# Picks as plain fp32 matmuls, and twelve picked slots instead of eleven, in a graph network on one core

## The reference

```python
# layer 0: two rounds of the mean over incoming edges
h = x @ W_lin + b_lin
agg1 = mean_aggregate(h, src, dst, N_NODES)          # mean of h[src] per dst
h = jnp.tanh(agg1 @ W1_agg + h @ W1_root + b1)       # 16 features
agg2 = mean_aggregate(h, src, dst, N_NODES)
out = jnp.tanh(agg2 @ W2_agg + h @ W2_root + b2)     # 64 features
# x = layernorm(x + out); layer 1: gated messages
h = x @ Wn.T + bn
w = ssp(ssp(edge_attr @ We1.T + be1) @ We2.T + be2)  # softplus - log 2
agg = segment_sum(h[src] * w, dst)
out = ssp(agg @ Wc.T + bc) @ Wp.T + bp
# result: layernorm(x + out)
```

## Time and profile before

| | |
|---|---|
| median of 3 runs | 8767.93 us (8767.54 to 8774.95) |
| profiled execution, first to last instruction | 8760.1 us (its own time beyond this span is not shown) |
| mean granted clock of TensorE | 0.951 of 2.4 GHz |
| TensorE matmuls, busy | 7637.1 us, 87% |
| GpSimd | 6259.5 us, 71% |
| ScalarE | 5860.1 us, 67% |
| VectorE | 5505.1 us, 63% |
| DMA | 392.62 MB, 45 GB/s over the span |

### The profile page before, as it was taken

How to read it: one execution, slowest core, us unless ns; L and a number is a source line. 1 busy time by engine, 2 the same in 40 slices (tenths; PEclk the granted TensorE clock), 3 DMA queues, 4 the chain that set the end, 5 groups by cost and what they waited for, 6 DMA issues and landing times. The chain is left out here.

```text
span 8760.1 us, 165117 instructions
## 1 busy us (share of the span) xinstructions
PE 7637.1 (87%) x51516; PEld 6905.6 (79%) x51517; DVE 5505.1 (63%) x7447; ACT 5860.1 (67%) x10176; POOL 6259.5 (71%) x6471
## 2 busy tenths in 40 slices
PE   7999999999989999999999777777777777888887
PEld 6999999888889999998888666666666666776775
DVE  5655656666645555556666666666666666777777
ACT  5777777666657777776666566666666666666665
POOL 5777777766557777777664477777777777777776
PEclk9999999999989999999999798988988889999999
DMA  2111112111111111111111222222222222222222
GB/s 75 35 34 35 35 34 35 31 30 28 25 40 34 35 34 35 34 34 31 31 30 23 75 56 59 55 57 57 55 58 56 55 59 55 55 59 56 55 56 59
DMA packets 341135, 392.62 MB, mean 45 GB/s; under 512 B 165119, under 2 KB 240563, under 8 KB 340564
## 3 DMA queue, kind: packets, MB, share of 16 engines
q0 software_dynamic: 204000, 151.96, 12.1%
q1 hardware_dynamic: 136750, 239.87, 8.1%
q10 hardware_dynamic: 322, 0.03, 0.0%
HBM read 375.47 MB, written 15.92 MB: 45 GB/s over the span
## 5 line engine op out<-in xcount | busy, mean ns | idle before, releaser
L699 PE MATMUL banks<-split_sb,e_low_hot 128*128 128x400 f32 x22000 | 4092.6, 346 | 45.6 <-DVE split_sb L752 45.6
L699 PEld LDWEIGHTS banks<-split_sb,e_low_hot 128*128 128x128 f32 x22000 | 4015.6, 189 | 74.1 <-DVE split_sb L752 46.1
L922 POOL DMA_INDIRECT big<-hn_table,src_i x2875 | 2857.0, 994 | 883.7 <-issue 870.7
L645 POOL DMA_INDIRECT big<-p_table,src_i x1750 | 1655.8, 946 | 695.2 <-issue 528.7
L758 DVE TENSOR_REDUCE picked<-banks 128x48 f32<-128x1200 f32 x1000 | 1300.1, 1300 | 1352.1 <-PE banks L699 1351.1
L670 ACT ACTIVATE e_low_hot<-e_key_off 128x1536 fp32r<-128x1536 f16 x1000 | 1381.1, 1381 | 1130.6 <-PE banks L699 1112.7
L645 POOL DMA_INDIRECT big<-h_table,src_i x1750 | 1674.9, 957 | 612.5 <-issue 529.6
L666 ACT ACTIVATE e_key_off<-e_key_in,node_off 128x384 f16<-128x384 f16 (+1 forms) x4000 | 2028.4, 577 | 125.5 <-DMA e_key_in<-sel_dram 41.4
L957 PE MATMUL banks<-hn_split,e_low_hot 128*128 128x448 f32 x7000 | 1500.1, 370 | 75.5 <-issue 70.1
L957 PEld LDWEIGHTS banks<-hn_split,e_low_hot 128*128 128x128 f32 x7000 | 1298.0, 188 | 217.1 <-issue 96.6
L781 DVE TENSOR_TENSOR hot<-e_dst_pair,banks 128x1536 bf16<-128x1536 bf16 (+1 forms) x934 | 931.1, 997 | 69.9 <-issue 0.6
(11 more groups left out here) (216 smaller groups left out, 4491.7 us busy)
## 6 DMA issues: line engine op xcount, KB each, us to landing
e_wide<-in_edge_t SPq DMA_DIRECT2D x125, 832.0 KB
e_key_in<-sel_dram SPq DMA_DIRECT2D x250, 343.8 KB
big<-hn_table,src_i POOLq DMA_INDIRECT x2875
big<-p_table,src_i POOLq DMA_INDIRECT x1750
big<-h_table,src_i POOLq DMA_INDIRECT x1750
e_key_in<-gate_dram SPq DMA_DIRECT2D x125, 64.0 KB
src_i<-in_src SPq DMA_DIRECT2D x375, 12.5 KB, 1.7
e_key_in<-sel_dram SPq DMA_DIRECT2D x250, 8.2 KB
```

What stands on the lines that cost most here:

```text
L645: pool.indirect_dma_start(buf[u][:, j, 0:ROW0], None, table, bass.IndirectOffsetOnAxis(ap=src_i[u][:, j:j + 1], axis=0),).then_inc(gathere ...
L699: last = pe.matmul(o, low_hot[gr][:, h, e], split_sb[:, part, h * HI1:(h + 1) * HI1, :], start=(h == 0 and part == 0), stop=(h == HI2 - 1 ...
L922: pool.indirect_dma_start(buf[u][:, j, 0:F], None, table, bass.IndirectOffsetOnAxis(ap=src_i[u][:, j:j + 1], axis=0),).then_inc(gathered[u ...
```

## The change

A pick becomes one matmul in plain fp32 where it was two in float32r. The tables are no longer split: split_sb becomes table_sb, hn_split becomes hn_all, and both are fp32. At the start of e1 and e2 the table is copied by place_table. In the normalising stage the bias addition writes into hn_all directly, the and and the subtraction on VectorE and the copy on ScalarE go, and the store to memory reads from hn_all. In e1 and e2 there are 12 picked slots, in four groups of three, and 13 gathered ones.

```diff
-SIZE = (3, 3, 3, 2)
+SIZE = (3, 3, 3, 3)
...
-        split_sb = mid.enter_context(nc.sbuf_tensor("split_sb", [P, 2, HI1 * HI2, H], F32R))
+        table_sb = mid.enter_context(nc.sbuf_tensor("table_sb", [P, HI1 * HI2, H], F32))
...
-                for part in range(2):
-                    dve.tensor_scalar(split_sb[:, part].rearrange("p (h a) f -> p h a f", h=HI2),
-                                      away[:, :, 0:HI1].unsqueeze(3).to_broadcast([P, HI2, HI1, H]),
-                                      1.0 - part, None, ALU.mult)
+                dve.tensor_copy(table_sb[:, :, :].rearrange("p (h a) f -> p h a f", h=HI2),
+                                away[:, :, 0:HI1].unsqueeze(3).to_broadcast([P, HI2, HI1, H]))
...
-            low_hot = [tiles.enter_context(nc.sbuf_tensor(f"{tag}_low_hot{gr}", [P, HI2, SIZE[gr] * P], F32R))
+            low_hot = [tiles.enter_context(nc.sbuf_tensor(f"{tag}_low_hot{gr}", [P, HI2, SIZE[gr] * P], F32))
...
-                                for part in range(2):
-                                    last = pe.matmul(o, low_hot[gr][:, h, e],
-                                                     split_sb[:, part, h * HI1:(h + 1) * HI1, :],
-                                                     start=(h == 0 and part == 0), stop=(h == HI2 - 1 and part == 1))
+                                last = pe.matmul(o, low_hot[gr][:, h, e], table_sb[:, h * HI1:(h + 1) * HI1, :],
+                                                 start=(h == 0), stop=(h == HI2 - 1))
...
-                    def split_table():
-                        tops, rests = [split_sb[0:PR, part].rearrange("p (h a) f -> p a h f", h=HI2) for part in range(2)]
-                        dve.wait_ge(split_in, 32)
-                        scratch = h1_deg[0:PR, :, :].rearrange("p n c -> p (n c)")
+                    def place_table():
+                        rows_of = table_sb[0:PR].rearrange("p (h a) f -> p a h f", h=HI2)
+                        dve.wait_ge(table_in, 32)
                         for h in range(2):
-                            at = slice(FULL_CUT[h], FULL_CUT[h + 1])
-                            top = scratch[:, HI2 * H * FULL_CUT[h]:HI2 * H * FULL_CUT[h + 1]].rearrange(
-                                "p (a h f) -> p a h f", h=HI2, f=H)
-                            dve.tensor_single_scalar(top.bitcast(I32), full_in[h].bitcast(I32), TOP12, ALU.bitwise_and)
-                            dve.drain()
-                            dve.tensor_copy(tops[:, at], top).then_inc(split_made, 1)
-                            dve.tensor_tensor(rests[:, at], full_in[h], top, ALU.subtract).then_inc(split_made, 1)
+                            dve.tensor_copy(rows_of[:, FULL_CUT[h]:FULL_CUT[h + 1]], full_in[h]).then_inc(table_made, 1)
...
-                            for part in range(2):
-                                for c in range(2):
-                                    last = pe.matmul(bank[c][:, 0:GHALF * F], low_hot[s][:, h, :],
-                                                     hn_split[:, part, h * GHIGH + c * GHALF:h * GHIGH + (c + 1) * GHALF, :],
-                                                     start=(h == 0 and part == 0), stop=(h == GLOW - 1 and part == 1))
+                            for c in range(2):
+                                last = pe.matmul(bank[c][:, 0:GHALF * F], low_hot[s][:, h, :],
+                                                 hn_all[:, h * GHIGH + c * GHALF:h * GHIGH + (c + 1) * GHALF, :],
+                                                 start=(h == 0), stop=(h == GLOW - 1))
...
-        hn_split = hn_held.enter_context(nc.sbuf_tensor("hn_split", [P, 2, NQ, F], F32R))
-        f_top = sem("f_top")
-        f_hi = sem("f_hi")
+        hn_all = hn_held.enter_context(nc.sbuf_tensor("hn_all", [P, NQ, F], F32))
...
                     dve.wait_ge(f_hn_psum, g + 1)
-                    if g >= 2:
-                        dve.wait_ge(f_store[g % 2], 16 * (g // 2))
-                    dve.tensor_tensor(hn_o[g % 2][:, 0:b - a, :], by_node(bank[5 + g % 2], b - a),
+                    dve.tensor_tensor(hn_all[:, a:b, :], by_node(bank[5 + g % 2], b - a),
                                       bn_all[:, :].unsqueeze(1).to_broadcast([P, b - a, F]), ALU.add).then_inc(f_out, 1)
-                    if g >= 2:
-                        dve.wait_ge(f_hi, g - 1)
-                    t = top_i[g % 2][:, 0:b - a, :]
-                    dve.drain()
-                    dve.tensor_single_scalar(t, hn_o[g % 2][:, 0:b - a, :].bitcast(I32), TOP12,
-                                             ALU.bitwise_and).then_inc(f_top, 1)
-                    dve.drain()
-                    dve.tensor_tensor(hn_split[:, 1, a:b, :], hn_o[g % 2][:, 0:b - a, :], t.bitcast(F32), ALU.subtract)
...
-                for g in range(NGQ + 3):
-                    if g < NGQ:
-                        a, b = group(g)
-                        act.wait_ge(f_xT_psum, g + 1)
-                        if g >= 2:
-                            act.wait_ge(f_hn_psum, g - 1)
-                        act.copy(x1T[g % 2][:, 0:(b - a) * F], bank[3 + g % 2][:, 0:(b - a) * F]).then_inc(f_xT, 1)
-                    if g >= 3:
-                        a, b = group(g - 3)
-                        act.wait_ge(f_top, g - 2)
-                        act.copy(hn_split[:, 0, a:b, :], top_i[(g - 3) % 2][:, 0:b - a, :].bitcast(F32)).then_inc(f_hi, 1)
+                for g in range(NGQ):
+                    a, b = group(g)
+                    act.wait_ge(f_xT_psum, g + 1)
+                    if g >= 2:
+                        act.wait_ge(f_hn_psum, g - 1)
+                    act.copy(x1T[g % 2][:, 0:(b - a) * F], bank[3 + g % 2][:, 0:(b - a) * F]).then_inc(f_xT, 1)
...
-                    sp.dma_start(hn_v[:, a:b, :], hn_o[g % 2][:, 0:b - a, :]).then_inc(f_store[g % 2], 16)
+                    sp.dma_start(hn_v[:, a:b, :], hn_all[:, a:b, :]).then_inc(f_store[g % 2], 16)
```

More of the change, by code:

```diff
@@ L13 @@
 F32 = mybir.dt.float32
-F32R = mybir.dt.float32r
 I32 = mybir.dt.int32
@@ L75 @@
 PICK = HI1 * H
-TOP12 = -4096
 BIG = 2.0 ** 126
@@ L587, in pick_phase @@
             pick_psum = sem(f"{tag}_pick_psum")
-            split_in = sem(f"{tag}_split_in")
-            split_made = sem(f"{tag}_split_made")
+            table_in = sem(f"{tag}_table_in")
+            table_made = sem(f"{tag}_table_made")
             pick_taken = sem(f"{tag}_pick_taken")
@@ L629, in _ @@
                                      [:, HI2 * FULL_CUT[h]:HI2 * FULL_CUT[h + 1], :].rearrange("p c f -> p (c f)")
-                                     ).then_inc(split_in, 16)
+                                     ).then_inc(table_in, 16)
                     keys(1, 1)
@@ L728, in body @@
                             pick(3, n + 1)
-                    pe.wait_ge(split_made, 4)
+                    pe.wait_ge(table_made, 2)
                     for gr in range(NGR):
@@ L815, in _ @@
                     dve.sem_inc(pick_taken, 2)
-                    split_table()
+                    place_table()
                     for gr in range(3):
@@ L843, in gate_phase @@
             key_in = [tiles.enter_context(nc.sbuf_tensor(f"{tag}_key_in{u}", [P, GSEL * P], F16)) for u in range(2)]
-            low_hot = [tiles.enter_context(nc.sbuf_tensor(f"{tag}_low_hot{s}", [P, GLOW, P], F32R)) for s in range(GSEL)]
+            low_hot = [tiles.enter_context(nc.sbuf_tensor(f"{tag}_low_hot{s}", [P, GLOW, P], F32)) for s in range(GSEL)]
             high = tiles.enter_context(nc.sbuf_tensor(f"{tag}_high", [P, GSEL, GHIGH], F32))
@@ L1307, in gnn_kernel @@
         x1, st_sum, st_mean, var, rstd, sq = norm_tiles("c")
-        tanh_w = [tiles.enter_context(nc.sbuf_tensor(f"tanh{b}", [P, GQ, F], F32)) for b in range(3)]
-        tanh_t = [t[:, 0:CQ, :] for t in tanh_w]
-        top_i = [t[:, :, :].bitcast(I32) for t in tanh_w[0:2]]
+        tanh_t = [tiles.enter_context(nc.sbuf_tensor(f"tanh{b}", [P, CQ, F], F32)) for b in range(3)]
         x1T = [tiles.enter_context(nc.sbuf_tensor(f"x1T{b}", [P, GQ * F], F32)) for b in range(2)]
-        hn_o = [tiles.enter_context(nc.sbuf_tensor(f"hn_o{b}", [P, GQ, F], F32)) for b in range(2)]
         def pack(t, k):
```

## The result

The changed kernel takes 13094.16 us (median of 4 runs, 13091.86 to 13095.38) against 8768.35 us: a ratio of 1.4928, 95% interval 1.4906 to 1.4949. The forecast was 13030 us. The profiled execution's span is 13092.2 us, 4332.1 us above that of before.

The account below looks back on a forecast made before the run. TensorE was taken to bound the edge phases, GpSimd's gathers the gate phase. Span 8760.1 + 4008 - 20 + 302 - 31 = 13019 us, with 7.8 us beyond the span 13027, put at 13030; range 12780 to 13450.

Parts of the forecast that it names:

- Picks in the edge phases: Edge phases: 48 plain fp32 matmuls replace 88 float32r ones, +16.0 us a block on TensorE, +4008 us over 250 blocks.
- The adding in the edge phases: Edge phases: the adding's waits for one-hots may shrink since VectorE is earlier, those between visits stay; -20 us.
- Gate phase: Gate phase: TensorE takes the lead from the gathers, 30.6 us a block plus extra visits; +302 us.
- hidden: Rival, gate phase: the gathers keep the pace and hide the dearer picks, 12730 us; chance 0.07.
- keeps its waits: Rival, gate phase: the adding still waits, 13230 us, or the product remains late, 13890 us; chance 0.05.
- Normalising stage: Stage before the gate phase: bitwise-and and subtraction go, GpSimd's addition comes next; about -25 us.
- Filling the table: Starts of both edge phases: two copies replace six operations in filling the pick table; -6 us.
- the time beyond the span: Whole kernel: the median of the runs was taken as 7.8 us above the profiled span.
- two passes: Rival, picks: a plain record costs what a float32r one does, 184 ns; about 9090 us; chance 0.04.
- dearer records: Rival, picks: each plain record also has float32r's 17 ns above its columns, +470 us, 13500 us; chance 0.07.
- faster: Rival, edge phases: a plain matmul costs one float32r matmul, so 13 gathers bound; 8250 to 8500 us; chance 0.02.

Follow-up runs that it names:

- few_before: The kernel before the change with 20 instead of 23 gathers in the gate phase, three slots' rows left out: 8306.7 us, ratio 0.9482.
- few_after: The changed kernel with 20 instead of 23 gathers in the gate phase, three slots' rows left out: 13092.82 us.
- one_part: The kernel before the change with twelve picked slots and only the top part picked in the edge phases (48 float32r matmuls a block): 8333.88 us, ratio 0.951.
- two_bf16: The kernel before the change, eleven slots, with edge-phase table parts and one-hots in bfloat16, lowest bits left out: 8760.6 us, ratio 0.9993.
- narrow_rest: The kernel before the change, second matmul of each edge-phase pair covering only 192 of 400 columns: 8733.09 us, a single execution.
- slot12: The kernel before the change with a twelfth picked slot in the edge phases, picks still in float32r: 9128.78 us, ratio 1.0414.
- plain11: The changed kernel with eleven instead of twelve picked slots in the edge phases, picks in plain fp32: 12357.21 us, ratio 1.4098.
- bf16_12: The kernel before the change with two bfloat16 parts in the edge phases, lowest bits left out, and twelve slots: 8747.09 us, ratio 0.9973.

## Why the prediction was right

The step that carried it was reading plain fp32's price off a row of another matmul in the same trace: two records a matmul and two passes a record. The changed kernel's pitch (from the start of one record to that of the next) of 337.9 ns for 400 columns is two passes of 166.7 ns and 4.6 ns. (The rule of the Trainium skill named in the prediction, FP8 and Floating Point Precision, TensorE Precision Notes, asks for four passes a matmul; by that rule, the trace agrees: 675.8 ns against 666.7.) Term by term:

- **Picks in the edge phases**, forecast +4008 us: measured +4127.6 (8220.2 less 4092.6). 337.9 ns a record in place of 335.5 makes 58 us of the difference. About all of the rest is the clock after the waits between visits, which was no term of the sum: by the clock records, the lower level costs the picks 94 us after the change (half of the 187 us that they spent at it) and 27 before.
- **The adding in the edge phases**, forecast -20: the busy time of L717 fell by 35, the idle time ahead of it from 209.1 to 190.6, -53 in all. The wait for one-hots is 46.6 us after 77.3; that between visits grew from 114.0 to 136.8.
- **Gate phase**, forecast +302: from the first record of the first layer to the end stage's first matmul it is 3745.7 us before (4957.04 to 8702.78) and 4033.0 after (9000.8 to 13033.8), +287. From the first pick to the last it is +302.2. The block of 30.3 us (forecast 30.6; 30.5 in the mean) and that of 34.7 (34.9; 34.8 in the mean) confirm the chain; `few_before` and `few_after` show that the lead changed, which the sum only argued. The rivals "hidden" and "keeps its waits" fall with the rows above.
- **Normalising stage**, forecast -25: 49.9 us from its first scaling to the gate phase became 33.3, -17. GpSimd's addition does come next, as forecast; it takes 1.46 us a group now.
- **Filling the table**, forecast -6: TensorE's wait for it went from 45.6 to 38.9 us.

4127.6 - 53 + 287 - 17 - 7 is 4338, the spans differ by 4332. So the forecast is 64 us short as a sum of larger misses that partly cancel: the picks and the adding of the edge phases cost 87 us more than forecast, the gate phase 15 less. The 7.8 us that the sum adds for the time beyond the span are too many as well: in every execution for which both numbers are kept, the time is about 2 us above the span. The rival *two passes* fell with the pitch, and so did *dearer records*: 4.6 ns above the columns, not 17. The rival *faster* was costed rightly as to its size (forecast 8250 to 8500; `one_part`, its stand-in, 8334), and its condition didn't hold.

One sentence of the prediction was wrong without harm: that GpSimd had slack beside TensorE in the edge phases. `two_bf16` shows that it hadn't. At one visit the 14 gathers (17.6 us) and TensorE (17.2) bind together: less work on TensorE gives nothing there (`two_bf16`, `narrow_rest`), and more of it is paid less what TensorE was already held up (`slot12`, 1.1 of 1.47 us). It did no harm here because the change adds 16 us a block, far beyond either. I read the sum of GpSimd's busy time, 30.38 of 40 us, and left out the 0.30 us ahead of each of 32 gathers: with them it is 40.

## What to carry to other kernels

Half the matmuls can be twice the time: count passes, and take the time of a pass from a row of the same trace that has the same type, per column and from start to start. Where two engines bind a stage together, an edit that loads one is paid nearly in full and one that relieves it gives nothing, so look at the busy time with the gaps between instructions before calling an engine free. Split the stage by kind of block, too: in `slot12` and `two_bf16` one-visit and two-visit blocks answer differently, and only their sum looks simple. And a relieved TensorE can lose clock, which hides a part of the relief.

## What the runs showed of the hardware

- One pass of 400 columns takes 169.2 ns in bfloat16 and 168.9 in plain fp32 (half of a record of 337.9), but 182 to 184 in float32r; at 448 columns 189.2 (half of 378.4) in plain fp32 and 209 in float32r. The cause of the surplus is open (`narrow_rest`).
- The record of a weight load of 128 columns is 188 ns long in float32r, 190 in plain fp32 and 98 in bfloat16.
- After waits of 1.5 and 0.5 us between short bursts TensorE's clock fell to its lower level for a few microseconds, in some two-visit blocks and not in others: 30 times an edge phase in the changed kernel, 29 in `slot12`, 11 in `plain11`, 8 or 9 before, 4 in `bf16_12`. In the changed kernel it cost up to 1.7 us a two-visit block. What decides is open.
